# Attention on one core: both PSUM pairs taken before the first of four row-strip matmuls

## What is computed

```
h  = layernorm(x)
q1, q2, k, v = h@Wq1, h@Wq2, h@Wk, h@Wv        # 16 heads of 32, 1024 tokens
for w, q in ((0, q1), (1, q2)):
    s   = causal(q @ k.T) / sqrt(32)
    y_w = softmax(s) @ v
y = y_0 - sigmoid(h@Wlam) * y_1
x = x + y @ Wo
```

## Time and profile before

| | before |
|---|---|
| median of 3 runs | 2149.22 us (2146.67 to 2152.12) |
| profiled execution: time | 2146.67 us |
| profiled execution: span | 2144.8 us |
| PE busy | 2065.8 us (96%) |
| DVE busy | 1270.5 us (59%) |
| POOL busy | 888.7 us (41%) |
| ACT busy | 855.0 us (40%) |
| mean granted TensorE clock | 0.989 of full |

### The profile page before, as it was taken

The page is one execution under the profiler, slowest core; times in us unless marked ns, Lnnn a source line. Parts: engine busy times, 40 slices in busy tenths (PEclk is TensorE's granted clock), DMA queues, the critical chain, the costliest instruction groups (busy, mean ns, idle before and its releaser), DMA issues.

```text
span 2144.8 us, 29394 instructions
## 1 busy us (share of the span) xinstructions
PE 2065.8 (96%) x11824; PEld 904.4 (42%) x11824; DVE 1270.5 (59%) x1838; ACT 855.0 (40%) x1304; POOL 888.7 (41%) x457
## 2 busy tenths in 40 slices
PE   7999999999999999999999999999999989999999
PEld 3444444444444444343434344343433333444444
DVE  5868677657755634455555555555556723675634
ACT  4434344334444322344343434343344442443431
POOL 3757585500000001676766565766756681000000
PEclk9999999999999999999999999999999998999999
DMA  7110111300000020000001010000000111000001
GB/s 230 35 34 30 30 35 33 139 0 1 1 1 1 1 61 12 1 16 16 16 11 21 11 21 1 16 16 16 1 11 6 38 52 40 0 1 20 20 1 40
DMA packets 68999, 55.53 MB, mean 26 GB/s; under 512 B 36800, under 2 KB 55232, under 8 KB 68608
## 3 DMA queue, kind: packets, MB, share of 16 engines
q1 hardware_dynamic: 61952, 41.07, 6.6%
q10 hardware_dynamic: 6912, 12.59, 1.9%
HBM read 43.02 MB, written 10.62 MB: 25 GB/s over the span
## 4 chain that ended last, share of the span: by engine, by line
PE 54%; POOL 4%; DVE 3%; ACT 3%; issue 1%; DVEq 0%; POOLq 0%; ACTq 0%
PE psum L116 9%; PE psum L1151 8%; PE psum L1239 8%; PE psum L1269 7%; PE psum L1299 5%; PE psum L140 5%; POOL b_totals L1523 3%; PE psum L1189 3%; PE psum L1245 2%; PE psum L1257 2%; PE psum L1282 2%; PE psum L1197 1%; PE psum L1275 1%; DVE b_maxima L1586 1%; ACT b_probs L1445 1%
## 5 line engine op out<-in xcount | busy, mean ns | idle before, releaser
L1523 POOL TENSOR_TENSOR b_totals<-b_totals,b_probs 128x2048 f32<-128x2048 f32 (+3 forms) x160 | 515.7, 3223 | 324.4 <-ACT b_probs L1445 318.7
L1586 DVE TENSOR_REDUCE b_maxima<-psum 128x2 f32<-128x1024 f32 (+3 forms) x384 | 350.7, 955 | 407.5 <-PE psum L1245 245.2
L1445 ACT ACTIVATE b_probs<-psum 128x1024 f32<-128x1024 f32 (+3 forms) x320 | 228.2, 765 | 269.4 <-PE psum L1282 168.9
L435 PE MATMUL psum<-hT,a_win 128*128 128x512 f32 x640 | 290.8, 597 | 0.8 <-ACT hT L555 0.8
L116 PE MATMUL psum<-hT,b_early 128*128 128x512 f16 x1024 | 229.2, 384 | 5.2 <-DVE b_middle L202 5.2
L116 PE MATMUL psum<-hT,W 128*128 128x512 f16 x1024 | 226.4, 381 | 3.9 <-DVE a_win L202 3.9
L435 PEld LDWEIGHTS psum<-hT,a_win 128*128 128x128 f32 x640 | 119.4, 191 | 129.4 <-issue 128.1
L116 PEld LDWEIGHTS psum<-hT,b_early 128*128 128x128 bf16 x1024 | 100.7, 99 | 132.7 <-issue 12.6
L116 PEld LDWEIGHTS psum<-hT,W 128*128 128x128 bf16 x1024 | 100.5, 98 | 126.4 <-DVE a_win L202 7.6
L1500 POOL MEMSET b_mask<- 128x128 f32 x1 | 0.2, 204 | 356.8 <-POOLq L267 356.8
L1633 DVE RECIPROCAL b_down<-b_down 128x128 f32<-128x128 f32 x128 | 112.0, 918 | 42.7 <-ACT b_down L1423 42.7
(11 more groups left out here) (225 smaller groups left out, 3295.7 us busy)
## 6 DMA issues: line engine op xcount, KB each, us to landing
a_parts<-in_w_guT ACTq DMA_DIRECT2D x32, 256.0 KB, 2.8
ternary<-W SPq DMA_DIRECT2D x1, 6144.0 KB, 18.0
a_win<-in_w_inT SPq DMA_DIRECT2D x20, 256.0 KB, 7.3
a_parts<-in_w_pT ACTq DMA_DIRECT2D x16, 256.0 KB, 2.6
b_down<-lam_rows SPq DMA_DIRECT2D x32, 128.0 KB, 2.8
b_early<-ternary SPq DMA_DIRECT2D x8, 512.0 KB, 8.1
out<-x SPq DMA_DIRECT2D x16, 256.0 KB, 2.2
x<-in_x SPq DMA_DIRECT2D x3, 1024.0 KB, 8.0
```

The costliest lines, as they stand in the source:

```text
L435: last = pe.matmul(ring(s, j), win[:, at:at + P], core["hT"][:, (i * KT + k) * BLK:(i * KT + k + 1) * BLK], start=(k == 0), stop=(k == KT ...
L1445: act.activation(held(u, s)[:, 2 * a:2 * a + 2, off:BLK], pair_banks(("score", u, s, a))[:, :, off:BLK], ACT.Exp, scale=SCALE).then_inc(ex ...
L1523: pool.tensor_tensor(acc, acc, held(u, s)[:, :, off:BLK], ALU.add).then_inc(summed, 1)
L1586: dve.tensor_reduce(maxima[u % 2][:, :].rearrange("p (h q c) -> p h q c", h=HPT, q=QT)[:, 2 * a:2 * a + 2, qt, kc], pair_banks(("row", u, ...
```

## The change

In `row` and in `scores` both pairs of PSUM banks are now taken before the first matmul of the set. Before, the second pair was taken between the second and the third matmul. The matmuls, their order, the number of waits and the values waited for are the same; only the place of the second wait in PE's order changes, in 384 sets (192 of rows, 192 of scores).

```
--- before.py
+++ after.py
@@ -1232,10 +1232,8 @@
                     pe.wait_ge(fill_copied, FREED_BY_ACT[NTH[("q", r, w, CQ - 1)]])
                 hi = min((kc + 1) * BLK, (qt + 1) * P)
                 width, diagonal = hi - kc * BLK, kc == qt // TPB
-                to = []
+                to = [take_pair(("row", u, n, a)) for a in range(2)]
                 for j in range(HPT):
-                    if j % 2 == 0:
-                        to.append(take_pair(("row", u, n, j // 2)))
                     last = pe.matmul(to[j // 2][:, j % 2, 0:width], strip(qT[w][r % 2], j, qt * P, (qt + 1) * P),
                                      strip(kT[w][r % 2], j, kc * BLK, hi), start=True, stop=not diagonal)
                     if j % 2 and not diagonal:
@@ -1262,10 +1260,8 @@
                 c, kt = STEPS[s]
                 r, w = divmod(u, 2)
                 off, diagonal = step_width(s), kt >= TPB * c
-                to = []
+                to = [take_pair(("score", u, s, a)) for a in range(2)]
                 for j in range(HPT):
-                    if j % 2 == 0:
-                        to.append(take_pair(("score", u, s, j // 2)))
                     pe.matmul(to[j // 2][:, j % 2, off:BLK], strip(kT[w][r % 2], j, kt * P, (kt + 1) * P),
                               strip(qT[w][r % 2], j, c * BLK + off, (c + 1) * BLK), start=True, stop=False)
                 if kt == 0:
```

## The result

The change made the kernel slower: 2173.88 us in the median of four runs (2168.71 to 2177.26), against 2149.32 for the kernel before (2146.67 to 2152.12, four runs). The ratio is 1.0109, with a 95% interval of 1.0087 to 1.0132. That is +24.6 us where +15 was forecast, and it lies above the forecast's range. The profiled execution took 2175.0 us, with a span of 2172.1.

The account below looks back on a forecast made before the run. PE, busy 96% of the span, was taken to bound the kernel. Six periods at 1.80 (10.8 us) and the terms outside them made +15.2 us, on the median 2164.4, said as 2164, with a range of 2153 to 2171.

Parts of the forecast that it names:

- units 13 and 14: Unit 13 up to 1647.6: +0.55; 1647.6 to 1675.8: 0, as GpSimd sets the time; unit 14: +0.8.
- unit 0: First unit of the attention layer: 10 late sets at 0.08 and 1.31 passed through once, +2.1 us.
- last unit: Sets of steps 4 and 5 each gate an exp before GpSimd runs without a pause: +0.65 us together.
- ten just-in-time sets: About ten more sets of a period come within 0.01 of being late: +0.05 us per period.
- The lateness itself: Late sets of a period: the second pair isn't released sooner, so nothing is regained, 0.
- The place of the wait: Late wait becomes PE's sequencer instruction: +0.08 us in each of 13 late sets, 1.04 per period.
- The early half's result, rows: Step 2, even unit: DVE can't start on the early row half, next score set later, +0.46 us per period.
- Scores: Early half's score result, step 5 of the odd unit: the exp starts later, +0.25 us per period.
- rival 4: More half clock as PE waits with nothing in flight: one further drop gives 2169, two 2174; chance 0.09.
- Rival 1: The late wait stays on its load, 0.01 replacing 0.08 per late set: +6.8 us, 2156; chance 0.19.
- Rival 2: No change: slack in DVE's and ACT's queues hides lost early results; +1 us, 2150; chance 0.10.
- rival 3: Faster by the clock: neither half-clock drop comes, saving up to 7.1 us, 2142; chance 0.04.

Follow-up runs that it names:

- swapped: The changed kernel with the second pair's wait put ahead of the first's in row and score sets; 2155.73 us, ratio 1.0032 to the kernel before.
- copies_early: The full change on top of the kernel before with ACT's copies of k split around two exps; 2159.29 us, ratio 1.0053 to the kernel before.
- from_unit1: The change against the kernel before, only from unit 1 on, with unit 0's rows and scores as before; 2171.55 us, ratio 1.0102.
- announce: The kernel before, with a row half without diagonal announced only behind the set, by the last matmul; 2155.26 us, ratio 1.0032.

## Why the prediction was off

The direction and the mechanism in the periods were right. Two terms of the sum were sized too small, the cover assumed for units 13 and 14 was not there, and one rival came true in one place. The span missed the forecast by 12.1 us (27.3 against 15.2): 4.3 of them lie in units 1 to 12, 3.1 in unit 0, 2.2 in units 13 and 14, 0.6 ahead of unit 0 and 0.3 in the last unit and behind it; 1.8 have nothing to do with the change. The medians, 24.6 apart, miss it by less. Per period, set by set from the two traces:

| term | forecast | measured |
|---|---|---|
| 13 late sets, place of the wait | 1.04 (0.08 each) | 1.36 (0.094 to 0.111 each) |
| ten just-in-time sets | 0.05 | 0.36 (0.034 to 0.038 each) |
| early row result, step 2 of the even unit | 0.46 | 0.47 |
| early score result, step 5 of the odd unit | 0.25 | 0.28 |
| sum | 1.80 | 2.47 |

*The lateness itself: 0.* Right. In the swapped kernel every set starts whole, and no time comes back for it.

*The place of the wait: +0.08 in each late set.* This is the step that failed, together with the term that hangs on it, and by its size only. The load does come 0.12 behind the release, as the earlier trace rows had it. What I read too cheaply is the end of the set, the "+0.01 since four loads queue up". I took the loads behind the instruction to follow one another as they do in a set whose waits stand on its loads, 0.007 apart. Behind the load at 1238.68 the second comes 0.036 later, and so all the rest is 0.03 later. 0.075 for the later load and 0.03 for the set behind it make 0.105. Why the second load comes so late isn't shown.

*"About ten more sets come within 0.01 of such lateness: +0.05."* I counted the sets rightly and gave them the wrong price, 0.005 each. They pay under 0.01 for the release, as I said, but they pay the 0.03 behind the first load too. The row set of step 2 of unit 5, after and before, on the timeline:

```profile
1156.23 1.08 ACT L1441 ACTIVATE b_probs<-psum 128x512 f32<-128x512 f32 x2 [0.46 <-PE psum L1278]
1156.94 0.34 PEld L1237 LDWEIGHTS psum<-b_middle 32*128 32x128 f32 x8 [0.63 <-issue]
```

```profile
1143.08 1.09 ACT L1445 ACTIVATE b_probs<-psum 128x512 f32<-128x512 f32 x2 [0.46 <-PE psum L1282]
...
1143.79 0.31 PEld L1239 LDWEIGHTS psum<-b_middle 32*128 32x128 f32 x8 [0.63 <-issue]
```

In both kernels the first of the two exps ends 0.11 us ahead of the load (at 1156.82 and 1143.68), and the load starts 0.71 after that exp's start. The release is past, but the way from it through the sequencer's instruction takes 0.12, so the instruction is still what the load comes behind. The loads span 0.34 in place of 0.31, and from this set on the kernel is 0.035 further behind. I had named this as what would make me wrong ("if separate waits cost also where they are already met") and given it no weight. Of the other sets, whose release is further back, none pays.

*The early half's result, rows.* Right to 0.01: DVE's reduction of step 2 starts at 1220.25, 1.40 later against the sets around it (forecast 1.4), and the next score set at 1221.59 is 0.55 later. *Scores.* The exp at 1170.17 starts 1.49 behind its set's loads and 0.28 later than before (forecast 0.25); the 0.03 are the late wait's again. In the even unit's step 5 ACT's copies covered the exp, as argued: there the row set moved by 0.007 beyond what the score set's wait had cost. `copies_early` shows the other side: with that cover taken away the same set pays 0.28.

*Unit 0.* Set by set it costs 5.15 us where I had 2.1. The terms above make 2.5 of them; the 1.31 of step 3 came out as 1.29 in `from_unit1`, where only the row ahead of that set is changed. The other 2.6 are the drop of the clock, which was rival 4 with its place wrong: not in a period but in unit 0. Whether the change or chance brought it stays open: three traces have it and nine haven't, one of each kernel. That the measured 2174 equals the time that rival 4 gave for two drops is luck.

*Units 13 and 14.* I let GpSimd cover all of 1647.6 to 1675.8 because it was busy 27.55 of 28.2 us. This wait was wrong. In that stretch PE's lag grew by 1.36 us set by set and only 0.81 were given back, at the end. GpSimd was full, but PE's chain was nearly as long (PE busy 26.53 of the 28.2); one engine's busy share next to 100% doesn't show slack in the others. Behind it, up to unit 15, the lag grew by 2.25, where I had 0.8; some 0.5 of that is a drop of the clock at 1703 (3.4 us long) that the kernel before hasn't.

*Which rivals.* Rival 1 is refuted by the 382 instructions and the load 0.12 behind its release; its own world was built in `swapped`, and its period of 121.9 came out as 121.99. Rival 2 falls with `announce`, rival 3 with every trace: the drops near 822 and 1760 to 1790 stayed.

*Readings that were off.* The row of the granted clock in the earlier trace rows has one slice below the rest, not two. Rival 4 said that the two drops before the change followed stretches of mostly idle PE; PE was busy 3.93 of the 5.2 us ahead of 819.2 and 3.88 of the 5.3 ahead of 1761.3. The last unit's terms add up to 0.67, not 0.65. None of these moves the forecast.

The Trainium skill ("TensorE: Matmul & The Clock Gate", The mechanism) has matmuls end in program order. `announce` fits it: there both halves are announced by the last matmul alone, and DVE starts on the first of them 1.18 us behind the late half's load (1209.96 to 1211.14), as it starts 1.18 behind the load of a whole set in the earlier trace rows. The ends of matmuls are modelled in the profile, so no run here tests their order itself.

## What to carry to other kernels

Take a resource as late as the code allows, and when two waits stand ahead of one instruction, put the one that ends last first in the code: here it was the one that stayed on the load (0.86 us a period lost, against 2.48 with the same two waits the other way round). A price worked out for late sets should be asked for the on-time ones too; ten times 0.036 us was as large an error as the one in the main term. And where sets are late, look for who releases late: two of four copies moved behind an exp on ACT gained 1.24 us a period, where both ways of taking the pairs first lost.

## What the runs showed of the hardware

A load behind a wait of the sequencer's own starts 0.12 us after the release (ACT's exp ends at 1238.56, the instruction stands from 1238.60 to 1238.65, the load comes at 1238.68); it is 0.05 with the wait on the load. The second load of a set behind such an instruction comes 0.036 behind the first, and 0.007 behind it where the instruction had ended at least 0.14 us before. Three of twelve traces, one of each kernel, have a drop of the granted clock to 0.50 for 6.8 us at 850. The drops elsewhere vary between executions of the same code: 3.4 or 6.8 us at 406, 6.8 or 10.2 near 822. By my estimate, half of such a difference of 3.4, that puts 1 to 2 us on any comparison of two single traces.
